# Two transformer layers on one core: softmax sums inverted packed as 128x32, output biases added early

## The reference, cut to what matters

```python
x = L0_attn_x                                   # (2, 512, 512)
for layer in (0, 1):
    xn = layernorm(x)
    x = x + attention(xn) + ffn(xn)             # ffn 0: rms norm with ln_w, 1792 wide; ffn 1: 1376 wide

def attention(xn):                              # 32 heads of 16, causal; layer 0 has 8 key/value heads
    q, k, v = ...                               # layer 1: v = xn @ Wv.T + bv
    scores = where(causal, q @ k.T, -inf) / 4
    weights = softmax(scores)                   # exp / sum of exp
    ctx = weights @ v
    return ctx @ Wo + bo                        # bo of 512: one bias per layer
```

## Time and profile before

| what | value |
|---|---|
| median of 3 runs | 890.82 us (888.83 to 896.04) |
| profiled execution, its own time | 892.07 us |
| its span, first to last instruction | 889.6 us |
| mean granted TensorE clock | 0.982 |
| PE busy | 832.2 us, 94% |
| DVE busy | 607.8 us, 68% |
| ACT busy | 462.0 us, 52% |
| POOL busy | 416.0 us, 47% |

### The profile page before, as it was taken

How to read it: one execution, slowest core, us unless ns; L and a number is a source line. 1 busy time by engine, 2 the same in 40 slices (tenths; PEclk the granted TensorE clock), 3 DMA queues, 4 the chain that set the end, 5 groups by cost and what they waited for, 6 DMA issues and landing times.

```text
span 889.6 us, 16314 instructions
## 1 busy us (share of the span) xinstructions
PE 832.2 (94%) x5611; PEld 629.0 (71%) x5612; DVE 607.8 (68%) x1584; ACT 462.0 (52%) x828; POOL 416.0 (47%) x551
## 2 busy tenths in 40 slices
PE   8889999989999898999998998999898998999995
PEld 4866666768867665777787865776578775666785
DVE  7756557797765968666877688575668766665545
ACT  2433555566644555545665465445465564544662
POOL 3233444446444653454443644454355545544543
PEclk9999999999999999999999999999999998999999
DMA  6672363534526263636564274656565384733231
GB/s 204 167 165 73 98 130 129 102 133 78 158 82 165 84 145 101 128 135 128 180 105 173 73 161 139 119 174 103 180 116 162 110 154 148 137 112 102 83 103 48
DMA packets 61841, 113.08 MB, mean 127 GB/s; under 512 B 8760, under 2 KB 11832, under 8 KB 61752
## 3 DMA queue, kind: packets, MB, share of 16 engines
q1 hardware_dynamic: 61760, 112.05, 49.1%
HBM read 87.30 MB, written 24.64 MB: 126 GB/s over the span
## 4 chain that ended last, share of the span: by engine, by line
PE 76%; DVE 15%; issue 3%; ACT 2%; POOL 2%; DMA 1%; POOLq 0%; SPq 0%; ACTq 0%; DVEq 0%
PE g_ring L1226 37%; PE acc L1226 21%; PE s_bank L1339 7%; PE g_ring L1379 6%; PE t_bank L1359 4%; DVE o_t L1215 4%; DVE s_bank L1196 3%; DVE h_lo L1175 2%; DVE x L1183 1%; DVE qk_parts L1134 1%; POOL x L955 1%; DVE context L1216 1%; DVE xn L1111 1%; PE g_ring L1263 1%; POOL w_lo L945 1%
## 5 line engine op out<-in xcount | busy, mean ns | idle before, releaser
L945 POOL TENSOR_TENSOR w_lo<-w_raw,w_hi 128x512 fp32r<-128x512 f32 x204 | 271.3, 1333 | 155.2 <-ACT w_hi L987 150.6
L1196 DVE CUSTOM_DVE_ANT_0 s_bank<-s_bank,causal 128x128 f32<-128x128 f32 (+3 forms) x512 | 236.9, 519 | 36.4 <-PE s_bank L1339 35.9
L967 POOL TENSOR_SCALAR_AFFINE_SELECT p<-p 128x256 f32<-128x256 f32 (+1 forms) x320 | 121.9, 382 | 295.3 <-ACT p L980 288.3
L1226 PE MATMUL g_ring<-xt_hi,w_hi 128*128 128x512 f32 (+1 forms) x504 | 210.8, 418 | 6.2 <-DVE xt_lo L1125 3.2
L1226 PE MATMUL g_ring<-xt_lo,w_hi 128*128 128x512 f32 (+1 forms) x504 | 199.2, 395 | 0.0
L1226 PE MATMUL g_ring<-xt_hi,w_lo 128*128 128x512 f32 (+1 forms) x504 | 198.4, 394 | 0.0
L980 ACT ACTIVATE p<-t_bank 128x512 f32<-128x512 f32 x320 | 173.8, 595 | 36.5 <-PE t_bank L1359 29.7
L987 ACT ACTIVATE w_hi<-w_raw 128x512 fp32r<-128x512 f32 x204 | 127.2, 628 | 112.9 <-PE g_ring L1226 77.7
L1226 PE MATMUL acc<-w_hi,h_hi 128*128 128x256 f32 (+1 forms) x528 | 157.0, 297 | 9.0 <-DVE x L1183 4.9
L1226 PE MATMUL acc<-w_lo,h_hi 128*128 128x256 f32 (+1 forms) x528 | 150.4, 285 | 0.0
L1226 PE MATMUL acc<-w_hi,h_lo 128*128 128x256 f32 (+1 forms) x528 | 150.3, 285 | 0.0
(11 more groups left out here) (86 smaller groups left out, 845.3 us busy)
## 6 DMA issues: line engine op xcount, KB each, us to landing
w_raw<-weights_in SPq DMA_DIRECT2D x204, 256.0 KB, 3.1
qk_scratch<-qk_parts SPq DMA_DIRECT2D x24, 512.0 KB, 2.9
q_op<-qk_scratch SPq DMA_DIRECT2D x96, 128.0 KB, 4.6
o_scratch<-o_t SPq DMA_DIRECT2D x32, 256.0 KB, 3.1
k_op<-qk_scratch SPq DMA_DIRECT2D x48, 128.0 KB, 7.0
context<-o_scratch SPq DMA_DIRECT2D x16, 256.0 KB
o_t<-o_scratch SPq DMA_DIRECT2D x16, 256.0 KB
k_op<-k_scratch SPq DMA_DIRECT2D x48, 64.0 KB, 5.4
```

What stands on the lines that cost most here:

```text
L945: pool.tensor_tensor(w_lo[:, c % SPLIT, :], w_raw[:, c % RAW, :], w_hi[:, c % SPLIT, :].bitcast(F32), ALU.subtract).then_inc(split_done, 1)
L967: pool.affine_select(out=view, in_=view, compare_op=ALU.is_ge, fill=0.0, base=0, pattern=[[0, n], [1, P]] if n == 2 else [[1, P]], channel ...
L1196: last = dve.tensor_tensor_reduce(out=bank[:, at:at + n], in0=bank[:, at:at + n], in1=causal[:, 512 - n:], scale=1.0, scalar=LOWEST, op0=A ...
L1226: ins = pe.matmul(dst, w[a], xa[c], start=first and i == 0, stop=last and i == 2, skip_group_check=skip)
```

## The change

- The sum rows are read back once, not 16 times: the eight heads' 512 sums as 128x32 into `sums`. DVE inverts those (`recip`, a step of its own), SyncE writes them to `r_scratch` (`rout`) and reads them spread over 16 partitions per head into `inverse`, 128x512 (`rin`); `norm` is the multiply alone.
- `o_t` is no longer a target of a read: its next copy waits for the last `o_scratch` write alone.
- The output biases are added to x by POOL as soon as a batch's last normalised tile is made (layer 0), or after the last V (layer 1); additions to x wait for that, where they follow it in the plan. The statistics of layer 1 and the stores follow the additions.
- One buffer, `bias_all`, holds the output bias of layer 0, then the bias of V, then the output bias of layer 1.
- The planner books: `recip` 0.45 and `norm` 0.75 for `norm` 1.3, `O_WRITE` 4, `O_READ` 8, `R_WRITE` 4, `R_READ` 5, `TAIL` 32, `O_AT` 10.5.

The diff, cut to its core:

```diff
--- before.py
+++ after.py
@@ -87,15 +87,17 @@
           "tanh": 0.5, "exp": 0.5, "oev": 0.5, "hhi": 0.53}
 DVE_US = {"stats": 3.2, "rstd": 1.1, "ms": 0.6, "rstd2": 1.2, "xn": 0.55, "xlo": 0.7, "qres": 0.68,
           "vsum": 0.62, "gsum": 0.61, "hmul": 0.61, "xadd": 0.62, "smax": 0.67, "mrow": 0.4,
-          "norm": 1.3, "hlo": 0.7}
+          "recip": 0.45, "norm": 0.75, "hlo": 0.7}
 POOL_US = {"wlo": 1.27, "xbias": 1.25, "mask": 0.42}
 SP_US = {"wload": 0.43, "losave": 0.4, "loback": 0.4, "qkout": 0.4, "qkin": 2.5, "kin": 2.5, "mout": 0.4, "min": 0.8,
-         "store": 0.43, "bo1": 0.43, "oout": 0.4, "oin": 1.0}
+         "store": 0.43, "bo1": 0.43, "bv": 0.43, "oout": 0.4, "oin": 1.0, "rout": 0.4, "rin": 0.5}
 US = {"pe": PE_US, "act": ACT_US, "dve": DVE_US, "pool": POOL_US, "sp": SP_US}
 SIGNAL = {"pe": 0.22, "act": 0.16, "dve": 0.15, "pool": 0.1, "sp": 0.1}
 TRANSFER = 2.5
 QK_WRITE, QK_READ = 8.0, 8.0
-O_WRITE, O_READ = 5.0, 10.0
+O_WRITE, O_READ = 4.0, 8.0
+R_WRITE, R_READ = 4.0, 5.0
+BIAS_READ = 8.0
 
 
 EARLY = 4.0
@@ -103,8 +105,8 @@
 LOAD_AHEAD = 25
 
 
-TAIL = 26.0
-O_AT = 10.0
+TAIL = 32.0
+O_AT = 10.5
 
 
 QK_AT = 0
@@ -212,6 +214,11 @@
             free = after("g", g - 2)
             xn = place("dve", max(at("stats", l, b, kind), after("xtr")), "xn", l, b, kind, tt, g, -1)
         e = end["xtr"] = pe_step(max(xn, free), "xtr", g, l, b, kind, tt)
+        end["xn_made", l, b] = after("xn_made", l, b) + 1
+        if l == 0 and end["xn_made", l, b] == (2 + b) * TT:
+            add_bias(l, b, xn)
+            if b:
+                end["bv"] = place("sp", max(v for k, v in end.items() if k[0] == "xbias"), "bv") + BIAS_READ
         hi = place("act", max(e, after("x_read", slot)), "xhi", g, kind, slot, tt)
         end["g", g] = end["x", slot] = place("dve", hi, "xlo", g, kind, slot, tt)
         if own is not None:
@@ -300,7 +307,11 @@
                 end["used", c] = end["x_read", xslot] = e
         used = at("PV", 2 * QUADS - 1) if (l, b) == (1, 1) else 0.0
         for i, x in enumerate(accs):
-            end["v", l, b] = end["acc", x] = place("dve", max(e, used), "vsum", x, l, b, part, i)
+            end["v", l, b] = end["acc", x] = place("dve", max(e, used, end["bv"] if l else 0.0), "vsum", x, l, b, part, i)
+        if (l, b, part) == (1, 1, 1):
+            here = place("sp", end["v", 1, 1], "bo1") + BIAS_READ
+            for batch in range(B):
+                add_bias(1, batch, here)
 
     def v_ready(xslot):
         a = state["acc"]
@@ -361,18 +372,24 @@
         if last:
             for i in range(2):
                 a = state["a"] + i
-                done = end["acc", a] = place("dve", e, "xadd", a, l, b, nh, i)
+                biased = end.get(("xbias", l, b, nh, i))
+                done = end["acc", a] = place("dve", max(e, biased or 0.0), "xadd", a, l, b, nh, i, biased is not None)
+                end["x_added", l, b, nh, i] = (done, a)
                 if ("group", ph, nh) not in end:
                     continue
-                done = end["x_final", l, b] = place("pool", max(done, after("bo1") if l else 0.0),
-                                                    "xbias", a, l, b, nh, i)
-                if nh == 0:
-                    end["x_final", l, b] = NEVER
+                end["x_final", l, b] = done if nh else NEVER
                 if l == 1:
                     place("sp", done, "store", a, b, nh, i)
-                elif b == 1 and nh == 1 and i == 1:
-                    end["bo1"] = place("sp", done, "bo1") + TRANSFER
             end["group", ph, nh] = e
+
+
+    def add_bias(l, b, ready):
+
+        for nh in range(2):
+            for i in range(2):
+                done, a = end.get(("x_added", l, b, nh, i), (0.0, -1))
+                done = end["xbias", l, b, nh, i] = place("pool", max(ready, done), "xbias", l, b, nh, i, a)
+                ready = max(ready, done + 2.0)
 
 
     def p_freed(j):
@@ -435,13 +452,15 @@
     def pv(u):
         g = take("g")
         e = end["PV", u] = pe_step(max(pv_ready(u), after("g", g - 2)), "PV", g, u)
-        end["g", g] = end["oev", u] = place("act", max(e, after("oout", u - 1) if u % 2 else after("norm", u // 2 - 1)),
-                                                      "oev", g, u)
+        end["g", g] = end["oev", u] = place("act", max(e, after("oout", u - 1)), "oev", g, u)
         octet = u // 2
-        end["oout", u] = place("sp", max(end["oev", u], after("norm", octet - 2)), "oout", u) + O_WRITE
+        end["oout", u] = place("sp", end["oev", u], "oout", u) + O_WRITE
         if u % 2:
-            free = max(end["oout", u], after("norm", octet - 1), after("split", "o", octet // KT - 1, 1, octet % KT))
-            here = place("sp", free, "oin", octet) + O_READ
+            free = max(end["oout", u], after("split", "o", octet // KT - 1, 1, octet % KT))
+            here = place("sp", max(free, after("rout", octet - 1)), "oin", octet) + O_READ
+            done = place("dve", here, "recip", octet)
+            end["rout", octet] = place("sp", done, "rout", octet) + R_WRITE
+            here = place("sp", max(end["rout", octet], after("norm", octet - 1)), "rin", octet) + R_READ
             end["norm", octet] = place("dve", here, "norm", octet)
 
     def w_early_ln(b, kind, slot, first):
...
@@ -899,16 +916,34 @@
                     if octet >= KT:
                         sp.wait_ge(hlo_done, split_of[("o", octet // KT - 1, 1, octet % KT)])
                     if octet:
+                        sp.wait_ge(r_out, 16 * octet)
+                    heads = o_scratch[octet % 2].rearrange("(j r) t -> j r t", j=8)
+                    sp.dma_start(sums[:, :], heads[:, HD, :].rearrange("j (a t) -> j a t", a=HD)).then_inc(o_here, 16)
+                    sp.dma_start(context[:, octet % KT, :], heads[:, 0:HD, :]).then_inc(o_here, 16)
+                elif kind == "rout":
+                    octet = s[1]
+                    sp.wait_ge(recip_done, n_recip[octet])
+                    if octet >= 2:
+                        sp.wait_ge(r_here, 16 * (octet - 1))
+                    sp.dma_start(r_scratch[octet % 2].rearrange("j (a t) -> (j a) t", a=HD), sums[:, :]
+                                 ).then_inc(r_out, 16)
+                elif kind == "rin":
+                    octet = s[1]
+                    sp.wait_ge(r_out, 16 * (octet + 1))
+                    if octet:
                         sp.wait_ge(norm_done, n_norm[octet - 1])
-                    heads = o_scratch[octet % 2].rearrange("(j r) t -> j r t", j=8)
-                    sp.dma_start(context[:, octet % KT, :], heads[:, 0:HD, :]).then_inc(o_here, 16)
-                    sp.dma_start(o_t[:, :], heads[:, HD:VW, :].to_broadcast([8, HD, T])).then_inc(o_here, 16)
+                    sp.dma_start(inverse[:, :], r_scratch[octet % 2].unsqueeze(1).to_broadcast([8, HD, T])
+                                 ).then_inc(r_here, 16)
                 elif kind == "bo1":
-                    sp.wait_ge(xbias_done, n_xbias_l0)
-                    sp.dma_start(bo_all[:, :], bo1.unsqueeze(0).to_broadcast([P, D])).then_inc(bo_here, 16)
+                    sp.wait_ge(acc_freed, v_made[(1, 1)])
+                    sp.dma_start(bias_all[:, :], bo1.unsqueeze(0).to_broadcast([P, D])).then_inc(bias_here, 16)
+                elif kind == "bv":
+                    sp.wait_ge(xbias_done, max(n for at, n in n_xbias.items() if at[0] == 0))
+                    sp.dma_start(bias_all[:, :], bv.unsqueeze(0).to_broadcast([P, D])).then_inc(bias_here, 16)
                 elif kind == "store":
                     _, a, b, nh, i = s
-                    sp.wait_ge(xbias_done, n_xbias[a])
+                    sp.wait_ge(xbias_done, n_xbias[(1, b, nh, i)])
+                    sp.wait_ge(acc_freed, n_acc_free[a])
                     sp.dma_start(out[b].rearrange("(t p) d -> p t d", p=P)
                                  [:, 2 * i:2 * i + 2, nh * HALF:(nh + 1) * HALF],
                                  x[:, b * TT + 2 * i:b * TT + 2 * i + 2, nh * HALF:(nh + 1) * HALF]
@@ -946,12 +981,14 @@
                                        w_hi[:, c % SPLIT, :].bitcast(F32), ALU.subtract
                                        ).then_inc(split_done, 1)
                 elif kind == "xbias":
-                    _, a, l, b, nh, i = s
-                    pool.wait_ge(acc_freed, n_acc_free[a])
-                    pool.wait_ge(bo_here, 16 * (l + 1))
+                    _, l, b, nh, i, a = s
+                    if a >= 0:
+                        pool.wait_ge(acc_freed, n_acc_free[a])
+                    pool.wait_ge(xn_done, x_last_xn[(l, b)])
+                    pool.wait_ge(bias_here, 48 if l else 16)
                     at = slice(b * TT + 2 * i, b * TT + 2 * i + 2)
                     dst = x[:, at, nh * HALF:(nh + 1) * HALF]
-                    bias = bo_all[:, nh * HALF:(nh + 1) * HALF].unsqueeze(1).to_broadcast([P, 2, HALF])
```

(70 more changed lines are left out.)

## The result

The changed kernel takes 862.9 us (median of 4, 862.3 to 864.6) against 891.2 (median of 4 of the kernel before): a ratio of 0.968, 95% interval 0.964 to 0.972. Forecast were 861 us, with a range of 849 to 880. Run again later it took 864.3 us (ratio 0.972, 0.968 to 0.976).

The account below looks back on a forecast made before the run. PE (TensorE) was taken as the bound, busy 832.2 of 889.6 us, idling mostly for DVE's row maxima. 892.07 - 22.8 (idle) - 11.8 (clock) - 1.8 (biases) + 5.4 (added steps) = 861.1, so 861 us; range 849 to 880.

Parts of the forecast that it names:

- The reciprocal's idle and clock: 128x512 reciprocal at L1215 cut to 128x32: PE gets back 22.8 us idle and 11.8 us of lost clock speed.
- rival 1: PE's idle time comes back but its clock doesn't, as a new order makes its own stalls: 873 us, chance 0.20.
- 2.74 us late behind every octet: DVE's reciprocal and multiply take 4.04 us where the planner books 1.3, so DVE runs 2.74 us late.
- The ratio of 0.52: Share of DVE's lateness that reaches PE as idle time: 1.42 us per octet of 2.74.
- rival 3: Slower: the second round trip (write and read of the inverse) stands in DVE's queue before the multiply; 922 us, chance 0.04.
- The small reciprocal: Reciprocal on 128x32 takes 0.35 us, bounds 0.18 and 3.34; with the multiply 1.04 us, within the 1.2 booked.
- PE's idle near 35 us: Expected sign in the changed kernel's profile: PE's total idle time near 35 us, from 57.4 before.
- The two more steps, +5.4: Added write and read of the inverse per octet: DVE waits 10.4 us for sums and inverse, costing PE 5.4 us.
- the waits for the sums: DVE waiting before the small reciprocal for the sums to land: five of 16 octets late, 5.4 us together.
- TAIL and O_AT: Planner constants raised (26 to 32, 10 to 10.5) to cover a last chain of 24.3 us instead of 16.6; taken 0.
- The biases: GpSimd's last two bias adds no longer stand before the final store, which follows DVE: -1.8 us; other adds 0.
- Replanning, +-5: The whole order is planned anew, so single stalls move: +-5 us without sign, kept for the range only.

## Why the prediction was right

The sum holds in its two halves too: PE's idle was to fall by 22.8 + 1.8 - 5.4 = 19.2 us and fell by 18.6, its busy time by 11.8 and fell by 11.0. That the total came within 2 us is in part luck, as new orders of one kernel moved it by 4 to 11 us in the runs above.

**The reciprocal's idle and clock: right, and the size holds.** 34.6 us were worked out, 34.0 measured with that instruction alone taken out (23.5 idle for 22.8, 10.1 busy for 11.8). The step that carried it was to take out of the 27.6 us what another releaser had caused, and to add the clock of the same stretches. A forecast from idle time alone would have been rival 1, 873 us, 10 above the measured time. The table of stretches saw six of the seven at the lower clock; the one at 707 us stands behind no reciprocal.

**Its explanation: open in one word.** "2.74 us late behind every octet" charged only what was not booked. The runs with truer bookings show that booking it is no cure, but not that lateness costs nothing. The ratio of 0.52 was fitted to the 2.74; put back whole, 3.35 us gave 0.56 idle per added us, and half of the columns 0.40. So one ratio does not hold for all lengths. DVE absorbed 1.5 us per octet in the first and 1.1 in the second, near the 1.3 that the prediction worked out under rival 3.

**The small reciprocal: right.** 346 ns for 350. The pair with the multiply was read as 1.04 us, by single multiplies of 0.69; by the means it is 0.346 + 0.887 = 1.23, so it just fills its booking. The sign "PE's idle near 35 us" left out the prediction's own +5.4 and -1.8; with them it is 38.2, and 38.8 was measured.

**The two more steps, +5.4: near in size, its reason not shown.** Without the reciprocal before had 857.6; less the 1.8 at the end that is 855.8, and the changed kernel measures 862.9 to 864.3, so all that was added costs 7 to 8.5 us. Of the terms, the waits for the sums were 5.0 us for 5.4, at four octets for five:

```profile
456.52 0.98 DVE L1212 TENSOR_TENSOR h_lo<-h,h_hi 128x512 fp32r<-128x512 f32 x1
460.06 0.35 DVE L1262 RECIPROCAL sums<-sums 128x32 f32<-128x32 f32 x1 [2.57 <-DMA context<-o_scratch]
```

This is the longest of them. The waits for the inverse were 0, for 5 us. Landings of o_scratch and then of the new r_scratch write:

```profile
DMA to landing us min/median/max: 2.0/2.8/8.7
...
DMA to landing us min/median/max: 1.4/2.1/3.0
```

The small write lands in 1.4 to 3.0 us, where I had taken m_scratch's 1.4 to 6.1: of the bounds the lower was right, and the estimate by the fit of the Trainium skill ("DMA: Bandwidth & Descriptors", Anatomy of one DMA), about 2 us, was the better one for this write. The rule of the shared ring (same page of the Trainium skill, Queues, rings and completion order), which spoke for rival 3, is not contradicted (o_scratch still takes up to 8.7), but no small write was held that long. The price of the waits, 0.52 of their length, is untested, as the run with O_READ 11 only moved them. In the profile the 7 to 8.5 us show as 4.9 us more idle than in the run without a reciprocal, spread over x, h_lo and maxima; which edit makes them is not settled. SyncE's longer queue, taken as 0, is one candidate: ACT's wait for weights rose from 4.4 to 10.9 us, and at 597 us the chain of the changed kernel holds 7.7 us of a weight load issued behind twelve reads of `qk_scratch`. PE's own list has no wait for w_lo, so a cost of it is not shown.

**TAIL and O_AT: wrong at 0.** With the old constants the changed kernel is 10 to 11 us slower, and over half of that is seen at the end, where the change itself made the chain longer; the rest can be the chance of another order. I had worked out that the last chain grows by 7.7 us, and priced the raise that covers it at nothing. That is right for the sum as a whole (chain and cover came together), but the text gave the reader no price for a missing cover.

**The biases: -1.8 local, nothing in the whole.** In the timeline the store does follow DVE directly:

```profile
855.78 1.41 DVE L1225 TENSOR_TENSOR x<-acc,x 128x512 f32<-128x512 f32 x2 [2.28 <-PE acc L1271]
...
849.76 7.89 SPq L947 DMA_DIRECT2D y_out<-x  x4
```

The last addition ends at 855.78 + 1.41 = 857.19 and the span 2.8 us later, as it did 2.6 us behind POOL's last add. In the run with this part alone the span also ends 2.7 us behind DVE's last addition. That this run shows no gain means that its new order took the 1.8 us back, or that they drown in the scatter of 887 to 897 us.

**Replanning, +-5.** Runs of the changed kernel with one or two constants changed are 4 to 11 us slower, none faster. A range of +-5 for a new order was too narrow; the range held because the bounds of other terms were wide.

## What to carry to other kernels

Price a long instruction on an engine that PE depends on by two things read behind each of its places: PE's idle time, less what others release, and the granted clock in the same stretch. Half the length cost 28% here, so the first half that is cut off pays most, until the clock stays up. Where a wait is booked away, look whether the next step waits instead. A change that lengthens a chain needs its cover at the end re-sized, and after that a planner's constants want a run of their own, for truer costs did not give a better order here.

## What the runs showed of the hardware

DVE's reciprocal goes by columns in one straight line: 173 to 178 ns at 4, 346 at 32, 944 at 128, 1753 at 256 and 3344 at 512, all on 128 partitions, about 6.2 ns per column. The 4096 sums of an octet cost 0.35 us as 128x32; with 16 copies of each, as 128x512, they cost 3.34.

The clock's share was larger than expected: with 3.35 us added at 16 places, PE's busy time was 27.4 us longer, nearly as much as its idle time, 30.2 us.
